# Writing the row maxima into the operand stacks from GpSimd's queue instead of SyncE's

## What is computed

```python
std_out = out_proj(softmax(where(mask, scores, neg)))
gsa_scores = scores + position_sensitivity * splat_attn
gsa_out = out_proj(softmax(where(mask, gsa_scores, neg)))
x = layernorm(x + (1 - blend) * std_out + blend * gsa_out)
h = silu(x @ w_gate) * (x @ w_up)
x = layernorm(x + sparsify_2to4(h) @ w_down)
```

## Time and profile before

| | us |
|---|---|
| median of three runs | 465.04 |
| lowest, highest | 464.11, 465.21 |
| the profiled execution | 464.35 |
| its span, first to last instruction | 462.6 |

### The profile page before, as it was taken

The page is one execution under the profiler, slowest core; times in us unless marked ns, Lnnn a source line. Parts: engine busy times, 40 slices in busy tenths (PEclk is TensorE's granted clock), DMA queues, the critical chain, the costliest instruction groups (busy, mean ns, idle before and its releaser), DMA issues.

```text
span 462.6 us, 6910 instructions
## 1 busy us (share of the span) xinstructions
PE 420.1 (91%) x2474; PEld 281.0 (61%) x2474; DVE 326.1 (70%) x926; ACT 231.6 (50%) x445; POOL 49.6 (11%) x47
## 2 busy tenths in 40 slices
PE   7699959634999999999999999999998989999992
PEld 6555645323656656656656656566554558888881
DVE  1678739842797896987986977978911446999925
ACT  1477520002756565656666655756677675444100
POOL 1353370000000000000000000079100000000000
PEclk9699975555999999999999999999999999999997
DMA  6045338993004925916908809760000000000002
GB/s 183 0 43 53 43 35 91 113 101 40 1 0 51 104 23 63 103 17 73 101 4 89 85 4 101 86 262 1 1 6 1 1 1 0 1 1 1 1 1 91
DMA packets 9810, 22.88 MB, mean 49 GB/s; under 512 B 3248, under 2 KB 7088, under 8 KB 7856
## 3 DMA queue, kind: packets, MB, share of 16 engines
q1 hardware_dynamic: 7680, 21.37, 36.1%
q10 hardware_dynamic: 2096, 1.07, 0.9%
HBM read 5.26 MB, written 1.05 MB: 14 GB/s over the span
## 4 chain that ended last, share of the span: by engine, by line
PE 76%; SPq 8%; ACT 5%; DVE 5%; DMA 2%; POOL 2%; issue 1%; ACTq 1%; DVEq 0%; POOLq 0%
PE ps L805 19%; PE ps L782 15%; PE ps L749 13%; SPq L349 8%; PE ps L728 6%; PE ps L628 5%; PE ps L630 5%; PE ps L629 5%; PE ps L811 3%; ACT pr L576 2%; PE ps L685 2%; PE ps L689 1%; PE ps L686 1%; PE ps L771 1%; DVE ps L1096 1%
## 5 line engine op out<-in xcount | busy, mean ns | idle before, releaser
L576 ACT ACTIVATE pr<-ps 128x512 f32<-128x512 f32 (+1 forms) x320 | 159.7, 562 | 143.3 <-PE ps L811 113.4
L1096 DVE CUSTOM_DVE_ANT_0 ps<-ps,causal 128x512 f32<-128x512 f32 (+3 forms) x256 | 145.4, 616 | 46.5 <-PE ps L749 46.1
L805 PE MATMUL ps<-s_st,k_st 100*128 100x256 f32 (+1 forms) x256 | 91.6, 360 | 13.7 <-DMA s_st<-m_t 13.7
L805 PEld LDWEIGHTS ps<-s_st,k_st 100*128 100x128 f32 x256 | 49.1, 192 | 75.1 <-ACT pr L576 51.3
L749 PE MATMUL ps<-k_st,s_st 96*128 96x256 f32 (+1 forms) x192 | 80.5, 423 | 8.6 <-DMA k_st<-feat_hik 8.4
L782 PE MATMUL ps<-pr,vx 128*32 128x512 f32 (+3 forms) x768 | 81.8, 498 | 0.6 <-ACT pr L576 0.4
L805 PE MATMUL ps<-q_st,k_st 100*128 100x256 f32 (+1 forms) x256 | 79.5, 313 | 0.0
L749 PE MATMUL ps<-k_st,q_st 96*128 96x256 f32 (+1 forms) x192 | 78.0, 408 | 0.0
L1089 DVE TENSOR_REDUCE mpart<-ps 128x2 f32<-128x256 f32 (+2 forms) x96 | 54.6, 596 | 9.7 <-PE ps L749 9.7
L805 PEld LDWEIGHTS ps<-q_st,k_st 100*128 100x128 f32 x256 | 49.3, 193 | 5.6
L749 PEld LDWEIGHTS ps<-k_st,s_st 96*128 96x128 f32 x192 | 40.9, 213 | 17.4 <-issue 9.1
(11 more groups left out here) (175 smaller groups left out, 541.8 us busy)
## 6 DMA issues: line engine op xcount, KB each, us to landing
q_st<-base_hiq SPq DMA_DIRECT2D x16, 128.0 KB, 4.0
s_st<-base_hiq SPq DMA_DIRECT2D x16, 128.0 KB, 5.5
q_st<-feat_hiq SPq DMA_DIRECT2D x16, 128.0 KB, 5.6
k_st<-base_hik SPq DMA_DIRECT2D x16, 128.0 KB, 5.5
k_st<-feat_hik SPq DMA_DIRECT2D x16, 128.0 KB, 5.4
x_sb<-_attn_hidden_states_dram SPq DMA_DIRECT2D x2, 512.0 KB, 4.6
q_st<-base_loq SPq DMA_DIRECT2D x8, 128.0 KB, 4.7
s_st<-base_loq SPq DMA_DIRECT2D x8, 128.0 KB, 5.5
```

The costliest lines, as they stand in the source:

```text
L576: act.activation(pr[:, s % NP, 2 * hh + vs[0]:2 * hh + vs[-1] + 1, first_q:end_q], src, ACT.Exp).then_inc(exp_done, 1)
L805: mm = pe.matmul(ps[:, bank, j * width:(j + 1) * width], k_st[b][0:SROWS, hh, kt * P:(kt + 1) * P], (s_st[b], q_st[b])[v][0:SROWS, hh, q:q ...
L1096: ins = dve.tensor_tensor_reduce(out=ps[:, slot, at:at + n], in0=ps[:, slot, at:at + n], in1=causal[:, BANK - n:BANK], scale=1.0, scalar=- ...
```

## The change

`maxima` leaves SP and becomes a function of GpSimd, with the same wait and the same two transfers. GpSimd now issues `maxima(p)` for each pair in order; the weight splits, which were its last work in one piece, are put in two halves: four pieces (those of `raw[0]`) after `maxima(5)`, four (those of `raw[1]`) after `maxima(6)`. SP keeps the stacks, the weight loads and the output.

```diff
@@ sync
-            def maxima(p):
-
-                sp.wait_ge(ring_free, ring_at[("turn_max", p)] + 1)
-                b = p % NB
-                sp.dma_start(q_st[b][MROW:MROW + 4, :, :].bitcast(F32), m_t[0:64, p % 2, :]).then_inc(m_loaded, 16)
-                sp.dma_start(s_st[b][MROW:MROW + 2, :, :].bitcast(F32), m_t[0:32, p % 2, :]).then_inc(m_loaded, 16)
-
...
             stack(1)
             stack(2)
-            maxima(0)
             for p in range(PAIRS):
-                if p + 1 < PAIRS:
-                    maxima(p + 1)
                 if p + 3 < PAIRS:
@@ gpsimd
-            for m, (n, src, hi, lo) in enumerate(slices()):
+            def split(m, n, src, hi, lo):
+
                 pool.wait_ge(raw_loaded[n], 16)
                 pool.tensor_scalar(hi, src, 1.0, 0.0, ALU.mult, ALU.add).then_inc(prep, 1)
                 pool.wait_ge(prep, 2 * m + 1)
                 pool.tensor_tensor(lo, src, hi.bitcast(F32), ALU.subtract).then_inc(prep, 1)
+
+            def maxima(p):
+
+                pool.wait_ge(ring_free, ring_at[("turn_max", p)] + 1)
+                b = p % NB
+                pool.dma_start(q_st[b][MROW:MROW + 4, :, :].bitcast(F32), m_t[0:64, p % 2, :]).then_inc(m_loaded, 16)
+                pool.dma_start(s_st[b][MROW:MROW + 2, :, :].bitcast(F32), m_t[0:32, p % 2, :]).then_inc(m_loaded, 16)
+
+            work = list(slices())
+            for p in range(PAIRS):
+                maxima(p)
+                if p in (PAIRS - 3, PAIRS - 2):
+                    first = len(work) // 2 * (p - PAIRS + 3)
+                    for m in range(first, first + len(work) // 2):
+                        split(m, *work[m])
```

## The result

The changed kernel takes 466.44 us (median of five runs, 465.38 to 466.75) against 464.43 us (464.04 to 465.21) for the kernel before in the same runs: a ratio of 1.0038 with an interval of 1.0021 to 1.0055. It is slower by 2.0 us. The forecast was a near even trade, -0.3 us, with 0.40 for slower. The span of the profiled execution goes from 462.6 to 464.7 us.

The account below looks back on a forecast made before the run. PE was taken as the bound behind a 13.7 us wait for pair 0's maxima. -9.8 + 7.5 + 2.0 = -0.3 us against the median 465.04 gave 464.7 us, range 460.8 to 471.

Parts of the forecast that it names:

- the price of the clock behind the new hole: After pair 6's hole: granted clock falls to 0.50, one restart costs 2.0 us, bounds 0 and 3.
- The gain of the first maxima: Pair 0: GpSimd issues its maxima 10.85 us earlier, PE goes on at 100.9, gain 9.8 us.
- What bounds the kernel, and the fixed period: Behind the first hole PE is the bound, period 33.19 us; moving pair 0 forward moves all behind it.
- x: What GpSimd adds against SP, from `m_t` to landing, for both transfers: taken as 1 us, between -1.2 and 2.5.
- The 4.93 us of SP's queue: Pair 0: SP's time from taking up the maxima (105.80) to PE going on (110.73), assumed for GpSimd's landing too.
- the 101.2: Pair 0: restart time after which the gain falls under the 9.5 us that pair 6 costs.
- The crawl through the stack packets: Rival, pair 0: small packets take turns with 8 KB stack packets, restart 104.5 to 109.7, 468 to 473.5 us; chance 0.25.
- The maxima of pairs 1 to 5 and 7: No effect: SP already issues within 0.03 us; slack 2.5 us, 1.9 for pair 7, hides x.
- The hole before pair 6: `maxima(6)` waits behind four splits, issued 9.07 us late; PE stands 7.5 us, bounds 5.3 and 9.
- The lock on GpSimd's descriptors: Caution on GpSimd's queue: DVE's two-port operations can lock out descriptor writing; DVE's longest put at 0.7 us.

Follow-up runs that it names:

- filled hole: The changed kernel with 28 additional products on PE ahead of pair 6's wait for its maxima, results overwritten: 461.45 us (0.9929).
- two splits ahead: The kernel before, with only the maxima of pair 6 moved to GpSimd, behind two splits: 467.76 us (1.0065).
- only pair 6 late: The kernel before, with only the maxima of pair 6 moved to GpSimd, behind the first four splits: 473.86 us (1.0207).
- changed, `stack(2)` held: The changed kernel, with SP holding stack(2) until the first maxima have landed: 463.04 us (0.9953).
- splits last: All maxima from GpSimd as in the changed kernel, but all eight splits behind maxima(7): 455.10 us, 0.9796 to the kernel before.
- pair 0 alone from GpSimd: The kernel before, with only pair 0's maxima issued from GpSimd, ahead of the untouched splits: 455.51 us (0.9803).
- late splits: The kernel before, with SP issuing maxima(0) ahead of stack(2) and GpSimd's splits starting once the last maxima are in m_t: 451.55 us (0.9710).

## Why the prediction was wrong

The step that failed is the price of the clock behind the new hole: 2.0 us with an upper bound of 3, measured 5.27. The gain of the first maxima was also too large, 9.8 us against 7.68 and 0.38.

*What bounds the kernel, and the fixed period:* right. What pair 0 gained reached pair 6 whole: -9.03 at both value products, and PE asks for pair 6's maxima at 301.92 instead of 310.92.

*The first maxima:* predicted 9.8 us, measured 7.68, and 0.38 from the clock coming back 3.7 us after the restart instead of 4.5. x, what GpSimd adds against SP, was right: 0.65 us until GpSimd takes the work up and 0.2 in landing make 0.85 against my 1. The term that was too small is what I added it to. The 4.93 us of SP's queue were taken as the traffic ended; beside traffic in full flow it is 6.5 to 7.6, from ACT's queue too. Without traffic it would have been a gain of about 11. Counted from the copy, PE went on 0.97 us later than the bare 102.08 says, at 103.05 in the times of before, past the 101.2 from which the prediction itself let the loss win.

*The crawl through the stack packets* fell as a mechanism. The rule of turns between queues, one packet at a time (the Trainium skill, "DMA: Bandwidth & Descriptors", section "Queues, rings and completion order"), doesn't by itself give a price: with 96 small packets or with 12 larger ones the pair took 6.7 and 6.5 to 7.6 us beside the traffic. What the traffic does to them, 2.6 to 3.6 us, is measured; how it does it is open.

*The maxima of pairs 1 to 5 and 7:* right, no wait, and the stretch over pairs 1 to 5 is as long as before (193.75 against 193.72 us).

*The hole before pair 6:* predicted 7.5 us, measured 7.04, by the very steps (305.18 for the end of the splits, landing 3.75 us behind).

*The clock behind it* is the failed step. I had priced one restart by another, that of pair 0, as if the slow stretch had one length. It had five (all in us; each row from one profiled execution):

| kernel | PE stood | slow after the restart | extra to the values |
|---|---|---|---|
| filled hole | 0.42 | 0 | 0.03 |
| two splits ahead | 2.05 | 3.4, from shortly after it | 1.43 |
| only pair 6 late | 7.43 | 4.9 | 2.18 |
| changed, `stack(2)` held | 6.89 | 9.4 | 4.13 |
| changed | 7.01 | 11.9 | 5.27 |

The last column is the time from PE's restart to the values at 318.30 before, less 7.38. The price is 0.42 to 0.44 us per slow us in the four with a slow stretch, and pair 0's restart, from which I took the 2.0, fits it (1.9 us for 4.5 slow ones); it's the stretch that differs, with the hole nearly the same in the last three. Why it lasts 4.9 us in one and 11.9 in another is open. All five runs of the changed kernel lie within 1.4 us, which speaks against chance from run to run there; the four runs of the kernel with only pair 6 late spread over 3.2 us.

*The -1.18 us* after it I had not in the sum at all: see the last section. With the terms as measured, -7.7 - 0.4 + 7.0 + 5.3 - 1.2 = +3.0; the early part's -0.97 makes it the +2.1 of the two profiles. With my 2.0 for the clock the same sum would be -0.2, close to the forecast -0.3, but by luck: the gain was 1.7 too large, and the hole, 0.5 too long, and the unforeseen 1.2 made up for it.

*The lock on GpSimd's descriptors* of which the Trainium skill, "SBUF — State Buffer", section "SBUF: two separate sides", warns did not show: GpSimd's two issues take 0.63 and 0.60 us, as SP's do, 0.79 at most. That VectorE's longest operations take 0.7 us was misread: `rw<-rec,blend` takes 1.17 in the kernel before, and in the feed-forward stage, where GpSimd issues nothing, `beats<-vx` takes 1.76.

## What to carry to other kernels

Before moving work to an idle queue, look where the moved step will stand in that queue's whole order, and lay its deadline beside the work ahead of it: here one piece in eight met a deadline of 5.5 us behind 9 us of work that nobody needed for another 60. If a queue is blocked by its own later work, reorder it first: one moved line gave about 12 us, the second queue at best 9.5. Other traffic belongs in the estimate: the two small transfers that take 3.9 us from GpSimd's issue to PE on idle queues took 6.5 to 7.6 beside the stacks. Price a hole on TensorE as its length plus about 0.44 us for each us that the granted clock stays at its lower level, and leave that length wide.

## What the runs showed of the hardware

GpSimd's work on the splits holds up some VectorE operations. In the kernel before, `rw<-rec,blend`, 128 by 16, takes 1.17 us where it meets a difference of two tiles (to 322.56) and 0.18 where it meets nothing; `attn<-otmp` takes 0.71 where it meets a copy to a high part (322.54 to 323.65) instead of 0.29. The kernel before:

```profile
321.03 1.53 POOL L463 TENSOR_TENSOR wu_lo<-raw,wu_hi 128x512 fp32r<-128x512 f32 x1
...
321.43 1.17 DVE L1121 TENSOR_TENSOR rw<-rec,blend 128x16 f32<-128x16 f32 x1
322.54 1.11 POOL L461 TENSOR_SCALAR wu_hi<-raw 128x512 fp32r<-128x512 f32 x1
323.09 0.71 DVE L1126 TENSOR_TENSOR attn<-otmp 128x128 f32<-128x128 f32 x1
```

The kernel with the splits last, at the same place:

```profile
311.97 0.18 DVE L1125 TENSOR_TENSOR rw<-rec,blend 128x16 f32<-128x16 f32 x1
312.64 0.29 DVE L1130 TENSOR_TENSOR attn<-otmp 128x128 f32<-128x128 f32 x1
```

Both read two operands in SBUF, and GpSimd's copy and difference read SBUF; `otmp<-ps,rw` between them, with one operand in PSUM, keeps its 0.42. The Trainium skill, "SBUF — State Buffer", section "SBUF: two separate sides", says just that of the port pair shared by VectorE and GpSimd: a VectorE instruction with two SBUF inputs contends with a GpSimd instruction that reads SBUF, and whichever starts first has the pair for the whole operation. The trace agrees.

From 318.30 to 330.66 DVE is busy for 11.39 of 12.36 us, so the 1.4 us reach PE: the changed kernel, whose splits end at 317.2, needs 11.18 us for this piece, the kernel before 12.36. Over the other kernels the piece grows with the delay of the two operations: 11.22 us with none (splits last), 11.89 with 0.95 (two splits ahead), 12.73 with 1.8 (pair 0 alone from GpSimd). In the kernel with the late splits `rw` is 0.17 there, but 0.72 and `attn` 1.25 later, where the splits now lie; from the values at 346.70 before to the end it takes 116.9 us against 115.9, so most of the gain is lost again there.
